# First experts' stage of a two-layer attention and mixture-of-experts kernel: fp16 halves and DMA transposes against fp32 products with the up weights stationary

## The reference, cut to what matters

```python
x = x + xattn0(layernorm(x), ctx, ...)
x = x + ffn0(layernorm(x), router_w, w1, w2, expert_scale)   # this stage
x = x + xattn1(layernorm(x), ctx, ...)
x = x + ffn1(layernorm(x), ...)

def ffn0(hidden_states, router_w, w1, w2, expert_scale):      # E=8, F=1024, D=256, TOPK=2
    probs = softmax(xf @ router_w.T)
    top_w, top_idx = top_k(probs, 2);  top_w = softmax(top_w)
    combine = sum(one_hot(top_idx, E) * top_w[..., None], axis=1)
    h = silu(einsum('td,efd->tef', xf, w1))
    y = einsum('tef,edf->ted', h, w2) * expert_scale[None, :, None]
    out = einsum('te,ted->td', combine, y)
```

## Time and profile before

| | us |
|---|---|
| three runs | 1653.68, 1654.06, 1657.20; median 1654.06 |
| the profiled execution, its own time | 1657.45 |
| its span (first to last instruction) | 1655.7 |
| PE busy | 1463.1 (88%) |
| DVE, ACT, POOL busy | 909.5, 850.2, 718.1 |
| mean granted TensorE clock | 0.954 of full |
| chain that ended last: PE's share | 80% |

### The profile page before, as it was taken

One profiled execution on the slowest core, in us unless ns is written; L12 is line 12 of the kernel. 1 busy time (PEld: TensorE's weight loads), 2 busy tenths in 40 slices (PEclk: granted clock), 3 DMA queues, 4 the chain that ended last, 5 costly groups with the idle time before them and its releaser, 6 DMA issues.

```text
span 1655.7 us, 41566 instructions
## 1 busy us (share of the span) xinstructions
PE 1463.1 (88%) x13358; PEld 1164.6 (70%) x13358; DVE 909.5 (55%) x2765; ACT 850.2 (51%) x2051; POOL 718.1 (43%) x1128
## 2 busy tenths in 40 slices
PE   6999999997279999999979999999983999999896
PEld 5777777765146666666658888888872798778796
DVE  4787777776422232223316777777762565555563
ACT  4766676664135555555535555555541444344452
POOL 4445666654543333333024555555536043332222
PEclk9999999999589999999989999999995899999998
DMA  4325545543159999999842433333223233333231
GB/s 127 113 91 94 107 112 67 113 88 48 32 117 177 205 192 175 179 176 176 161 115 87 90 89 86 95 88 92 86 67 80 78 119 110 115 95 97 92 118 53
DMA packets 289089, 182.17 MB, mean 110 GB/s; under 512 B 212575, under 2 KB 267425, under 8 KB 288933
## 3 DMA queue, kind: packets, MB, share of 16 engines
q1 hardware_dynamic: 266580, 144.22, 40.7%
q0 software_dynamic: 18608, 32.14, 7.4%
q10 hardware_dynamic: 3744, 3.70, 0.8%
HBM read 99.10 MB, written 35.80 MB: 81 GB/s over the span
## 4 chain that ended last, share of the span: by engine, by line
PE 80%; issue 7%; DVE 5%; DMA 3%; ACT 2%; POOL 2%; another core or an unknown queue 1%; ACTq 1%; DVEq 0%; SPq 0%; POOLq 0%
PE psum L2224 13%; PE psum L1518 10%; PE psum L1505 10%; PE psum L1852 7%; PE psum L2237 7%; PE psum L1927 3%; PE psum L1858 3%; PE psum L899 2%; PE psum L1901 2%; PE psum L1918 2%; PE psum L1013 2%; PE psum L975 2%; PE psum L924 2%; PE psum L892 2%; PE psum L994 2%
## 5 line engine op out<-in xcount | busy, mean ns | idle before, releaser
L2224 PE MATMUL psum<-d_xT,d_w 128*128 128x256 f16 (+1 forms) x2304 | 241.2, 261 | 19.0 <-issue 16.7
L1443 DVE SCALAR_TENSOR_TENSOR b_h<-b_hid,b_h 128x1024 f16<-128x1024 f32 x71 | 87.0, 1225 | 277.7 <-ACT b_h L1471 276.9
L2224 PEld LDWEIGHTS psum<-d_xT,d_w 128*128 128x128 f16 x2304 | 203.7, 100 | 46.9 <-issue 23.3
L1505 PE MATMUL psum<-arena,b_xT 128*128 x852 | 198.4, 384 | 28.6 <-DMA b_xT<-b_x 27.3
L1518 PE MATMUL psum<-arena,b_hT 128*128 x1704 | 201.4, 275 | 14.8 <-DMA b_hT<-b_h 9.9
L1518 PEld LDWEIGHTS psum<-arena,b_hT 128*128 128x128 f16 x1704 | 166.4, 98 | 54.2 <-issue 21.6
L1505 PEld LDWEIGHTS psum<-arena,b_xT 128*128 128x128 f16 x852 | 84.0, 99 | 119.1 <-issue 35.8
L2277 ACT ACTIVATE d_sg<-psum 128x256 f32<-128x256 f32 (+1 forms) x192 | 65.5, 348 | 175.1 <-PE psum L2224 155.9
L1354 POOL DMA_INDIRECT b_xg<-dram_normed,b_gi x71 | 67.1, 944 | 197.9 <-DVE b_x L1436 186.2
L1466 ACT ACTIVATE b_hid<-psum 128x512 f32<-128x512 f32 x142 | 84.5, 597 | 126.9 <-PE psum L1505 79.4
L2321 DVE SCALAR_TENSOR_TENSOR d_hf<-psum,d_sg 128x256 f32<-128x256 f32 (+1 forms) x192 | 70.8, 379 | 143.3 <-ACT d_sg L2277 114.4
(11 more groups left out here) (288 smaller groups left out, 3218.7 us busy)
## 6 DMA issues: line engine op xcount, KB each, us to landing
d_wst<-in_L_w SPq DMA_DIRECT2D x64, 384.0 KB
stage<-in_L_w SPq DMA_DIRECT2D x32, 512.0 KB, 6.5
dram_expert_rows<-b_ys SPq DMA_DIRECT2D x71, 128.0 KB
ctxT<-in_ctxT SPq DMA_DIRECT2D x64, 128.0 KB, 3.7
dram_normed<-xn SPq DMA_DIRECT2D x64, 128.0 KB
x<-in_x SPq DMA_DIRECT2D x32, 128.0 KB, 5.3
dram_x<-xnew SPq DMA_DIRECT2D x32, 128.0 KB
c_xres<-dram_x SPq DMA_DIRECT2D x32, 128.0 KB
```

What stands on the lines that cost most here:

```text
L1443: dve.scalar_tensor_tensor(out=h16[:, p, 1, :], in0=hid[:, p, :], scalar=H_SCALE, in1=h16[:, p, 0, :], op0=ALU.mult, op1=ALU.subtract).the ...
L1505: i = pe.matmul(psum[:, 1 + 2 * p + half, :], xT[:, j % NT, px, c, :], weights(e, c, pw, half * 512, 512), start=(n == 0), stop=(n == len( ...
L2224: i = pe.matmul(psum[:, q, m * n:(m + 1) * n], w16[:, fc % RING, pw, col:col + P], xT[:, p, px, c, at:at + n], start=(k == 0), stop=(k == ...
```

## The change

The first experts' stage computes in fp32 throughout. What the code now does:

- `arena` holds the fp32 weights (the same 128 KB a partition; an fp32 value takes the room of two fp16 halves). SP loads each chunk straight to its place (`load_weights`), and `high` and `low` are gone.
- Per block, the two w1 chunks of its expert are copied to a fixed buffer `wup` of two slots, chunk 0 by ACT and chunk 1 by DVE (`copy_up`). Both engines now read the expert number themselves.
- The gathered rows are transposed by PE (`transpose_x`, two matmuls against the identity) and copied from PSUM by DVE (`xT_out`).
- `up` has the weights stationary and the activations moving: 8 chunks of F by 2 chunks of D, 16 fp32 matmuls of 128 x 128 columns. Its product is already transposed, so Silu's output goes to `hT` directly, and no DMA transpose is left.
- `down` has `hT` stationary and the w2 rows moving, 8 fp32 matmuls of 256 columns.
- `y_out` moves from ACT to DVE. PE's order in one turn is `up(j + 1)`, `transpose_x(j + 3)`, `down(j)`.

```diff
-        SHARED, WEIGHTS, WORK = 14 * 1024, E * CH0 * 2 * F * 2, 67424
+        SHARED, WEIGHTS, WORK = 14 * 1024, E * CH0 * F * 4, 67424
...
-        arena = region(SHARED, WEIGHTS)("arena", [P, E * CH0 * 2 * F], F16)
+        arena = region(SHARED, WEIGHTS)("arena", [P, E * CH0, F])
...
-                def load_stage(b):
-                    if inside(b):
-                        if due(b - 1):
-                            sp.wait_ge(stage_lo, b - 1)
-                        sp.dma_start(stage[:, b % 2, :], chunk(a["L0_w"], b)).then_inc(stage_ld[b % 2], 16)
+                def load_weights(b):
+                    if inside(b):
+                        sp.dma_start(arena[:, b, :], chunk(a["L0_w"], b)).then_inc(first_w, 16)
...
-                    high(b)
...
-                    low(b)
...
-            x16 = sa("x16", [P, NT, 2, D], F16)
-            xT = sa("xT", [P, NT, 2, DC, P], F16)
-            hid = sa("hid", [P, 2, F])
-            h16 = sa("h16", [P, 2, 2, F], F16)
-            hT = sa("hT", [P, 2, 2, FC, P], F16)
+            xT = sa("xT", [P, NT, DC, P])
+            wup = sa("wup", [P, 2, DC, F])
+            hT = sa("hT", [P, 2, FC, P])
...
+            def weights(e, c, at, n):
+                return arena[:, :, :].rearrange("p c f -> p (c f)")[:, bass.ds(e * (CH0 * F) + c * F + at, n)]
+            def expert_of(eng, j):
+                return eng.value_load(etab[0:1, j:j + 1], min_val=0, max_val=E - 1)
...
-                            pool.wait_ge(xlo_ready, j - NX + 1)
+                            pool.wait_ge(xt_done, j - NX + 1)
...
+                def xT_out(j):
+                    if inside(j):
+                        dve.wait_ge(xt_done, j + 1)
+                        if due(j - NT + 1):
+                            dve.wait_ge(up_done, 2 * (j - NT + 1))
+                        dve.tensor_copy(xT[:, j % NT, :, :].rearrange("p c t -> p (c t)"), psum[:, 5 * (j % 2), 0:D]).then_inc(xT_ready, 1)
+                def y_out(j):
...
+                        dve.tensor_copy(ys[:, p, :], psum[:, 6 + p, 0:D]).then_inc(y_ready, 1)
+                def copy_up(j):
+                    if inside(j):
+                        e = expert_of(dve, j)
...
+                        if due(j - 1):
+                            dve.wait_ge(up_done, 2 * (j - 1))
+                        dve.tensor_copy(wup[:, j % 2, 1, :], weights(e, 1, 0, F)).then_inc(wup_ready[1], 1)
+                for j in range(-3, N_B):
+                    copy_up(j + 2)
+                    xT_out(j + 3)
+                    y_out(j)
...
+                        for half in range(2):
+                            act.wait_ge(up_done, 2 * j + half + 1)
+                            act.activation(hT[:, p, half * 4:half * 4 + 4, :].rearrange("p f t -> p (f t)"), psum[:, 1 + 2 * p + half, :],
+                                           ACT.Silu).then_inc(silu_done, 1)
...
+                        act.activation(wup[:, j % 2, 0, :], weights(e, 0, 0, F), ACT.Copy).then_inc(wup_ready[0], 1)
...
+                        pe.wait_ge(xT_ready, j + 1)
+                        for c in range(DC):
+                            pe.wait_ge(wup_ready[c], j + 1)
+                        for f in range(FC):
+                            half, q = f // 4, f % 4
+                            if q == 0 and due(j - 1):
+                                pe.wait_ge(silu_done, 2 * (j - 2) + half + 1)
+                            for c in range(DC):
+                                i = pe.matmul(psum[:, 1 + 2 * p + half, q * P:(q + 1) * P], wup[:, p, c, f * P:(f + 1) * P], xT[:, j % NT, c, :],
+                                              start=(c == 0), stop=(c == DC - 1))
...
+                        for f in range(FC):
+                            if f % 4 == 0:
+                                pe.wait_ge(silu_done, 2 * j + f // 4 + 1)
+                            i = pe.matmul(psum[:, 6 + p, 0:D], hT[:, p, f, :], weights(e, 2 + f // 4, (f % 4) * D, D),
+                                          start=(f == 0), stop=(f == FC - 1))
...
-                for j in range(-1, N_B + 1):
-                    up(j + 1)
-                    down(j - 1)
+                for j in range(-3, N_B):
+                    e = expert_of(pe, j) if inside(j) else None
+                    up(j + 1)
+                    transpose_x(j + 3)
+                    down(j, e)
...
-                        sp.dma_start_transpose(xT[:, p, :, :, :].rearrange("p h c t -> p (h c) t"),
-                                               x16[:, p, :, :].rearrange("p h d -> p (h d)")).then_inc(xT_ld[p], 16)
...
-                        sp.dma_start_transpose(hT[:, p, :, :, :].rearrange("p h c t -> p (h c) t"),
-                                               h16[:, p, :, :].rearrange("p h f -> p (h f)")).then_inc(hT_ld[p], 16)
```

More of the change, by code:

```diff
@@ L169, in at_col @@
             return t[:, b:b + 1] if isinstance(b, int) else t[:, bass.ds(b, 1)]
-        def piece(t, b, part):
-            o = b * (2 * F) + part * F
-            return t[:, o:o + F] if isinstance(o, int) else t[:, bass.ds(o, F)]
         def due(v):
@@ L1489, in b_pe, with transpose_x @@
                 pe.wait_ge(t_ready, 1)
-                expert = {}
-                def weights(e, c, part, at, n):
-                    return arena[:, bass.ds(e * (CH0 * 2 * F) + (c * 2 + part) * F + at, n)]
+                def transpose_x(j):
+                    if inside(j):
+                        pe.wait_ge(g_ld[j % NX], nth(j, NX))
+                        if due(j - 1):
+                            pe.wait_ge(xT_ready, j - 1)
+                        for c in range(DC):
+                            i = pe.transpose(psum[:, 5 * (j % 2), c * P:(c + 1) * P], xg[:, j % NX, c * P:(c + 1) * P], ident[:, :])
+                        i.then_inc(xt_done, 1)
                 def up(j):
@@ L1497, in up @@
                         p = j % 2
-                        e = expert[j] = pe.value_load(etab[0:1, j:j + 1], min_val=0, max_val=E - 1)
-                        pe.wait_ge(xT_ld[j % NT], nth(j, NT))
-                        if due(j - 1):
-                            pe.wait_ge(silu_done, 2 * (j - 1))
-                        for half in range(2):
-                            terms = [(a_, b_, c) for c in range(DC) for a_, b_ in ((0, 0), (0, 1), (1, 0))]
-                            for n, (px, pw, c) in enumerate(terms):
-                                i = pe.matmul(psum[:, 1 + 2 * p + half, :], xT[:, j % NT, px, c, :], weights(e, c, pw, half * 512, 512),
-                                              start=(n == 0), stop=(n == len(terms) - 1))
-                            i.then_inc(up_done, 1)
@@ L1509, in down @@
-                def down(j):
+                        pe.wait_ge(xT_ready, j + 1)
[5 more added lines that the diff above has]
+                                pe.wait_ge(silu_done, 2 * (j - 2) + half + 1)
+                            for c in range(DC):
+                                i = pe.matmul(psum[:, 1 + 2 * p + half, q * P:(q + 1) * P], wup[:, p, c, f * P:(f + 1) * P], xT[:, j % NT, c, :],
+                                              start=(c == 0), stop=(c == DC - 1))
+                            if q == 3:
+                                i.then_inc(up_done, 1)
@@ L1510, in down @@
+                def down(j, e):
                     if inside(j):
                         p = j % 2
-                        e = expert.pop(j)
-                        pe.wait_ge(hT_ld[p], nth(j))
+                        if j == 0:
+                            pe.wait_ge(first_w, 16 * E * CH0)
                         if due(j - 1):
                             pe.wait_ge(y_ready, j - 1)
-                        terms = [(c, a_, b_) for c in range(FC) for a_, b_ in ((0, 0), (0, 1), (1, 0))]
@@ L1517, in down @@
-                        for n, (c, ph_, pw) in enumerate(terms):
-                            i = pe.matmul(psum[:, 6 + p, 0:D], hT[:, p, ph_, c, :], weights(e, 2 + c // 4, pw, (c % 4) * D, D),
-                                          start=(n == 0), stop=(n == len(terms) - 1))
+                        for f in range(FC):
[3 more added lines that the diff above has]
+                                          start=(f == 0), stop=(f == FC - 1))
@@ L1548, in store @@
                         sp.dma_start(tile(ys_d, j), ys[:, j % 2, :]).then_inc(y_st[j % 2], 16)
-                for j in range(-3, N_B + 2):
-                    transpose_h(j)
-                    store(j - 2)
-                    transpose_x(j + 3)
-                    if j == N_B - 4:
+                for j in range(N_B):
+                    store(j)
+                    if j == N_B - 6:
                         first_rows(sp)
```

104 lines of the change are left out of this document (32 added, 72 removed).

## The result

The changed kernel takes 1797.81 us (median of 4 runs, 1791.14 to 1801.67). The kernel before took 1653.87 us beside it (median of 4, 1645.4 to 1657.2). The ratio is 1.0875, with an interval of 1.0823 to 1.0927. The forecast was 1774 with a range up to 1790: the direction was right, the time lies outside the range. The two profiled executions differ by 1799.9 - 1655.7 = 144.2 us of span, where the sum had 118.6.

A forecast was written before the change was run, and what follows sets the result against it. PE was taken to bound the kernel, alone on the experts' stage's steady chain. 1657.45 + 119.6 (stage) - 1 (first attention) = 1776.0 us, put at 1774 for the runs' lower median; range 1762 to 1790.

The forecast's parts named there:

- The price of a block: Experts' stage: `up` 3.58, transposes 0.22 and `down` 3.46 us make 7.26 us a block, 2.05 more than 5.21.
- the prediction's own trial: Experts' stage: weight loads added in series would make `up` about 7.0 us and the stage some 240 us longer; not adopted.
- Rivals 2 and 3: Experts' stage: fp32 weight loads pace `up`, 1965 us, 2%; or an fp32 product costs one record, 1524 us, 2%.
- No wait in the turn: Experts' stage: copies, Silu and expert-number reads fit beside PE; ACT does 2.24 of 7.26 us; no wait added.
- Rival 1: Experts' stage: PE waits for the copied weights, a turn takes 8.5 us, 92 us more, 1867 us; 3%.
- 26.6 us put down to start and end: Experts' stage before: 396.5 us less 71 blocks at 5.21 us, said to hang on DMA transposes.
- No DMA at the end: End of the experts' stage: the last `down` no longer waits for a DMA transpose (4.25 us before).
- rival 4: Whole kernel: release of ACT, DVE and the DMA queues repays the loss, needing 119 us; 1%.
- The first attention, a gain of 1 us, between 0 and 8: First attention: 32 copies leave ACT and 32 operations leave DVE; gain 0 to 8 us, taken as 1.
- The signs of being wrong: Block's turn outside 7.1 to 7.4 us, `wup` copies or number's read in the chain, attention ending over 8 us earlier.
- The 4.7 us in five "issue" waits: Start of the experts' stage, first `down` calls: perhaps due to the transposes' traffic; counted 0, up to 5 us.
- What follows the stage moves along: After the experts' stage: store and second attention's gather hang on the same chain and shift with it, nothing added.

The follow-up runs named there:

- e8: Changed kernel with ACT's copy of w1 chunk 0 done three times instead of once: 1806.95 us, ratio 1.0886.
- e7: Changed kernel with half of the `down` product left out (4 of 8 fp32 products a block): 1683.98 us, ratio 1.0146.
- e5: Changed kernel, unaltered, run and traced again: 1813.88 us, ratio 1.0932.
- e6: Kernel before, unaltered, traced a second time: 1660.63 us, ratio 1.0019.
- e14: Changed kernel with an extra, unread DVE operation per attention block where `low` stood, on the late kind of chip: 1798.63 us, ratio 1.0792.
- e15: Changed kernel with the attention's scatters issued one block per turn over four turns, on the late kind of chip: 1793.25 us, ratio 1.0792.
- e13: Changed kernel, unaltered, a third time, as baseline on the late kind of chip: 1812.95 us, ratio 1.0891.
- e16: Changed kernel with gathers held to at most three blocks ahead, on the late kind of chip: 1799.58 us, ratio 1.0807.
- e4: Kernel before with 31 of 32 `low` operations left out and the low halves cleared once at the start: 1616.73 us, ratio 1.0053.
- e12: Kernel before with the scatters spread over four turns: 1599.44 us, ratio 0.9964.
- e17: Kernel before with scatters spread over four turns and gathers held to three blocks ahead: 1599.26 us, ratio 0.9946.
- e2: Changed kernel with gathers held to at most three blocks ahead, on the hardly late kind of chip: 1730.01 us, ratio 1.0758.
- e3: Changed kernel with scatters spread over four turns, on the hardly late kind of chip: 1731.59 us, ratio 1.0769.
- e10: Changed kernel with scatters spread over four turns, again on the hardly late kind of chip: 1730.83 us, ratio 1.0791.
- e11: Changed kernel with gathers held to at most three blocks ahead, again on the hardly late kind of chip: 1733.08 us, ratio 1.0808.
- e18: Changed kernel with scatters spread over four turns and gathers held to three blocks ahead: 1731.69 us, ratio 1.0778.

## Why the prediction was right and wrong

**The price of a block: right.** 7.26 forecast, 7.245 measured, each of the three terms within 0.01 us. fp32 products of the second attention were the right rows to read the earlier trace rows. Over 71 blocks it is 1.07 us less than forecast, so this step is out of the miss. An fp32 load of 128 columns is recorded with 194 ns and 32 records take 3.57 us, so the loads lie beside the products. The Trainium skill (TensorE: Matmul & The Clock Gate, "LDWEIGHTS") has a load at its columns over 1.2, an estimate of 107 ns for 128; the 194 ns recorded disagree. To add a load in series to each record was the prediction's own trial, and the 0.112 us a record speak against it. Rivals 2 and 3 fell with these numbers.

**No wait in the turn: right.** DVE's copy of the weights took 0.69 us (0.5 to 2 forecast), PE's read of the expert number 0.30 to 0.49 us, ahead and hidden; e8 showed that 2.1 us more on ACT change nothing, e7 that PE is the only bound. Rival 1 fell. The 5.21 us a block of the kernel before were read from undisturbed turns; its fifty blocks average 5.31, so about 7 of the 26.6 us put down to start and end lay in the steady part. The sum didn't use them.

**No DMA at the end: right.** Nothing stands ahead of the last `down`. The DMA share fell to 0.14, and that repaid nothing: rival 4 fell.

**The first attention, a gain of 1 us, between 0 and 8: wrong, in sign. This is the step that failed.** It took 17 us more (16 in e5 against e6). The step failed at "everything that PE waits for stands ahead of these copies in its engine's order". That is true of the order, and yet PE's wait for ACT's `attT` grew from 4.3 to 15.6 us, since the `pT` ahead of it started late. I asked only who waits for the removed operation, not whom it holds up. `low` stretched POOL's scatters, and on this kind of chip PE and the readers of its products come late while POOL's rows run without that. The signs of being wrong named only an attention that ends earlier, not one that ends later. Shown on the chip: putting the DVE work back takes the lateness from 20.1 to 7.9 us, PE's wait for `attT` from 17.3 to 5.7 and the scatter blocks from 187.7 to 163.9 (e14); spreading the rows takes the lateness to 10.7 and the attention down by 31.5 us (e15, more than repeats differ). The lateness explains 12 of the 17 us, in the second pair 7 of 16. But the scatter blocks hold all of both (20.3 and 19.2 us more), so the rest stands beside the scatters too. Repeats of one attention differ by up to 15.6 us. The 7.2 us that came back between the last block and the first gather belong to a stretch that takes 38.9 to 45.2 us with the same code (e13, e7); I have no cause for it.

**The 4.7 us in five "issue" waits, counted as 0 with up to 5: mis-sized.** The stall lasted 8.8 us and the clock fell in it, together 10.3 us (7.6 in `up(1)`, 0.2 in the transposes, 2.1 in `down(0)`, 0.4 in `up(0)`). I took the 26.6 us of start and end as wholly due to DMA transposes. In fact the kernel before had the same halting rhythm at 467.0 to 473.4 us, while POOL issued gathers, and it stayed when the transposes went. e16 shows whose it is in the kernel after: with the gathers paced the start takes 31.7 instead of 41.2 us. For the kernel before that was not run on this kind of chip.

**What follows the stage moves along: 5.0 us short, not shown to be the change's.** It took 5.0 us more here and 6 in e5 against e6. But it takes 806.5 to 812.4 us in the kernels with the change on this kind of chip, and 801.7 and 807.4 in the two traces of the kernel before. On the other kind it takes 766.4 to 768.1 us with the change and 766.5 to 768.8 in e4, e12 and e17, without it. No run was made for it; the cause is open.

**On the other kind of chip** the forecast's size is close. There e2, e3, e10, e11 and e18 stand 123.6 to 127.2 us above the kernel before, where the difference forecast was 118.6. The unaltered kernel after was not run there: each of the five has paced gathers, spread scatters or both.

**The range** had the start's loss up to 5 us and no loss at all in the attention. Some 17 us for the attention and 10 for the start would have had to stand in it. Of the waits that nothing in the program explained, those of the earlier trace rows were a sign of it. Those of the earlier trace rows were not: PE's "issue" waits before the same transposes came to 7.6 us before (20 to 420 us) and 7.2 after.

## What to carry to other kernels

Ask of a removed operation not only who waited for it, but also what it slowed: it may have been the brake on something that hurts the bounding engine. An "issue" stall without a cause may belong to what runs beside it; look at what POOL does at the same microseconds before you put it down to the part that goes. For fp32 products take the pace of a row of records in the chain, not a record's duration, and don't let one engine's indirect DMAs run further ahead than they are needed.

## What was unexpected of the hardware

- While POOL issued gathers of 0.95 us every 1.25 us, PE's records came by ones to threes, 0.8 us each in the mean (11 records of `up(1)` in 8.8 us), with nothing to wait for. In the block shown of the attention the start of `pT` came 1.4 us later than before (2.43 against 1.03 us behind the scores).
- This happened on one kind of chip only: lateness 17.7 to 23.3 us with unaltered scatters there, 1.1 and 4.8 in e2 and e11 on the other kind. The kernel before differs by 3% between them (1654 to 1663 against 1606 us), and the part behind the last `down` by 33 to 46 us (802 to 812 against 766 to 769). That lies in the second experts' stage: from PE's first product there to its last it takes 370 to 379 us against 335 to 336, while the second attention takes the same 389 to 394 us on both. PE's "issue" waits in that stage come to 21.5 us in the kernel before and 2.3 in e17. What differs in the chips, how POOL's DMAs reach PE, and whether it is the issuing or the transfers that does, stays open.
- A DVE operation of 1.22 us with two 128x1024 operands stretched a scatter of POOL from 0.97 to 1.84 us.
- 192 to 196 ns weight loads in fp32 lie fully beside 128-column products at 0.112 us a record.
